# A two-layer graph network on one core: the residual pieces of h, the zero fills, the first search step and the tile words

## The chip, the cores and the metric

The program runs on one core of a Trainium2 chip. The time is the device time of one execution in microseconds (us); the runs before gave 5438.78 us as the median of three (5437.1 to 5440.79).

## The reference

`x` is a table of 12500 nodes by 64 values, `src` and `dst` are 412500 edges, sorted by `dst`. LN is a layer norm without weights (eps 1e-5).

```
h    = relu(LN(x))
x1   = x + relu(h @ W_self + mean over the edges into a node of h[src] @ W_neigh + b)
h    = relu(LN(x1))
e    = sigmoid(relu([h[src], h[dst]] @ We1 + be1) @ We2 + be2)      # one gate per edge
m    = e * h[src]
msgs = [segment_max(m, dst), segment_sum(m, dst)]
out  = x1 + relu([msgs, h] @ Wn1 + bn1) @ Wn2 + bn2 + h
```

`h + ...` in the last line is the residual inside the second network, and `x1 + ...` the outer one.

## The kernel before, in words

The nodes lie in T = 98 tiles of P = 128. Each engine has a program of its own, and the order of the work is written out by hand with semaphores; nothing is planned by a scheduler. A loop made by `in_one_block` is a loop on one engine. The stages in order of time:

- **Search (0 to 180 us).** For each node the place of its first edge in `dst` is sought. ScalarE (L1577, loop of SITER = 10 steps of PASS = 10 columns, entered after `act.wait_ge(s_q, 2)`) counts with Sign activations in which row of 625 entries the place lies. VectorE turns the counts into row numbers (`rows_of`, L954 and L955; `stage_rows`, L958), GpSimd gathers these rows (L580), and VectorE counts inside them (`count`, L964). `search_step(it)` first takes all ten columns of step it + 1 with one `rows_of`, then counts step it, two columns at a time, and stages the rows of the next. It is called for step 0, in a loop with the moments of x (L981), and once behind it. Before and beside it the SP queue brings x (L742, L743) and copies `src` (L746 to L749).
- **Sort (180 to 380 us).** GpSimd gathers each node's list of sources (L580, `runs`), 14 halves of 7 tiles; VectorE masks each half (L1042, L1045, L1047), sorts the first 32 entries (L1055, L1059) and writes it (L1064, L1065). SP stores each half to `sorted_rows` (L761). Two halves stand ahead of a loop and two behind it. At the start SP waits for `s_start` and fills `extra_rows` (L751) and `ranked_rows` (L753) with zeros from SBUF.
- **h and its pieces.** ScalarE makes h of layer 0 in 14 groups (L1606), rounds each to bf16 as the first piece (L1611) and stores h (L1612). The second piece is the rounded rest, the third the rounded rest of the rest: GpSimd subtracts (L602), ScalarE rounds (L1616), GpSimd subtracts again (L607), each for two halves of 49 tiles. In GpSimd's program they stand behind all gathers of the sort. Only the sums of layer 0 (L1867) use the pieces.
- **Ranking (380 to 440 us).** VectorE counts how many sources of each node lie in early tiles (L1094, L1095), bins the nodes by how many are left, and ranks them by a one-hot matrix of 64 bins by 98 tiles (L1111), a scan (L1113), and its product with the offsets (L1128, L1130) summed over the bins (L1131). `row_at` (L1141) lets GpSimd scatter the rows by rank (L613, 98 scatters).
- **Tile words (440 to 455 us).** On one partition VectorE works out per tile how many slots and blocks it has and where they begin (`word_sums`, `rounded_up`, L1149 to L1195), into `ctl`. Then it raises `s_ctl`, for which SP (ahead of the first edge load of layer 0), GpSimd and TensorE wait.
- **Layer 0 (455 to about 2170 us).** 49 steps q of two phases. VectorE builds one-hot matrices of source ids (L1286), TensorE makes counts of them (L1859), ScalarE evicts these (L1627), TensorE multiplies them with the pieces of h (L1867), and the node part follows (`mean_of` L1292 to L1299, `new_x` L1305, `new_h`). The one-hot matrices of a phase begin only when TensorE has transposed the next ids (L1849), which in turn waits until the phase before has been built. VectorE's steps 0 to 4 are written out, the rest are loops. From step 5 on the words of the tiles serve to pack the late rows (`take_late`, L1253). SP loads the late rows and the ids of the early ones (`load_late`, L829) between `next_tiles(4)` and `next_tiles(5)`.
- **Behind it** GpSimd gathers the rest of the early rows (to 2430 us), then layer 1 runs tile by tile to the end.

## Time and profile before

| | |
|---|---|
| median of 3 runs | 5438.78 us |
| the profiled execution | 5435.6 us |
| its span | 5433.9 us |
| VectorE busy | 4035.2 us (74%) |
| GpSimd busy | 3687.3 us (68%) |
| ScalarE busy | 2774.4 us (51%) |
| TensorE busy, matmuls | 2013.7 us (37%) |
| mean granted TensorE clock | 0.697 |

A share is an average over stages that have different limits; what an edit is worth is read from its own stage. In a row of the timeline the first number is the start, the second the duration, then engine (PE TensorE, DVE VectorE, ACT ScalarE, POOL GpSimd, SPq the queue of SP) and line, and in brackets the time for which the engine was idle just before and what ended it; "issue" is a wait for nothing that the profile shows. The granted clock of 1.00 is 2.4 GHz and 0.50 is 1.2 GHz; between them it is a mean of stretches at the two.

### The profile page before, as it was taken

The numbers are of one execution on the slowest core, as the hardware profiler recorded it, in microseconds if no ns is written. First come the engines' busy times: TensorE is split into PE (matmuls) and PEld (weight loads), VectorE is DVE, ScalarE is ACT, GpSimd is POOL, SyncE is SP. The second block draws the span as 40 slices with busy tenths as digits, with TensorE's granted clock in tenths as the row PEclk, the third lists the DMA queues.
The fourth block names the chain that finished last, engine by engine and source line by source line (L and its number), as shares of the span: only waits on it lengthen the run. The fifth ranks groups of instructions, "written<-read, shape, count | busy, mean of one in ns | idle before, by whom it ended". The sixth has DMA issues, their size and how long they took to land.

```text
span 5433.9 us, 105141 instructions
## 1 busy us (share of the span) xinstructions
PE 2013.7 (37%) x18241; PEld 1777.4 (33%) x18241; DVE 4035.2 (74%) x8508; ACT 2774.4 (51%) x7285; POOL 3687.3 (68%) x3830
## 2 busy tenths in 40 slices
PE   0005899999999998000111111111111111111110
PEld 0004888888888888000000000101011111111110
DVE  6788788888888886006777778878888888887770
ACT  7304777887888886003444444444445444544440
POOL 5545216777777777767777777777777777766547
PEclk9999999999999999555555555555555555555555
DMA  7610315555555555554434444444444444443440
GB/s 212 166 24 27 41 52 173 160 160 158 163 160 160 158 163 167 158 156 101 124 113 124 124 122 125 124 133 126 132 133 135 133 142 136 142 134 118 123 98 24
DMA packets 491280, 696.11 MB, mean 128 GB/s; under 512 B 249885, under 2 KB 339843, under 8 KB 491163
## 3 DMA queue, kind: packets, MB, share of 16 engines
q0 software_dynamic: 181472, 381.28, 26.1%
q1 hardware_dynamic: 228085, 172.05, 10.3%
q10 hardware_dynamic: 81638, 141.95, 7.8%
q14 instruction: 69, 0.57, 0.0%
q8 instruction: 16, 0.26, 0.0%
HBM read 513.68 MB, written 163.18 MB: 125 GB/s over the span
## 4 chain that ended last, share of the span: by engine, by line
PE 22%; issue 20%; POOL 19%; DVE 17%; DMA 8%; ACT 7%; ACTq 4%; DVEq 3%; POOLq 0%; SPq 0%
POOL counts_f L580 13%; PE ps_acc L1867 10%; PE ps L1859 9%; DMA counts_f<-early_rows 5%; POOL extra_f L580 4%; DVE act_w L1450 4%; ACT counts_f L1627 3%; DMA counts_f<-hA_table,stage 2%; DVE pre L1444 2%; DVE run_max L1467 2%; ACT msg L1726 1%; DVE z L1456 1%; POOL out_dram L727 1%; ACTq L1726 1%; DVE pre L1059 1%
## 5 line engine op out<-in xcount | busy, mean ns | idle before, releaser
L580 POOL DMA_INDIRECT counts_f<-hA_table,stage x2144 | 2070.9, 966 | 794.3 <-issue 632.1
L1627 ACT ACTIVATE counts_f<-ps 128x784 bf16<-128x784 f32 x1568 | 1269.3, 823 | 468.6 <-PE ps L1859 385.7
L1444 DVE TENSOR_TENSOR pre<-counts_f,ps 128x512 f32 (+1 forms) x862 | 588.6, 683 | 825.2 <-SPq L897 316.9
L580 POOL DMA_INDIRECT extra_f<-hA_table,estage x984 | 932.1, 947 | 314.4 <-issue 290.4
L1726 ACT ACTIVATE msg<-counts_f,gate (+1 forms) x3448 | 921.5, 337 | 315.9 <-ACT gate L1721 293.8
L1867 PE MATMUL ps_acc<-pieces_f,counts_f 128*128 128x192 bf16 x9604 | 1021.3, 247 | 2.4 <-issue 2.4
L1867 PEld LDWEIGHTS ps_acc<-pieces_f,counts_f 128*128 128x128 bf16 x9604 | 885.7, 138 | 3.3 <-issue 2.8
L1859 PE MATMUL ps<-hot 128*128 128x196 bf16 x6272 | 820.6, 253 | 127.0 <-ACT counts_f L1627 106.5
L1938 PE MATMUL ps_acc<-ident,h_tile 128*64 128x128 f32 x98 | 38.6, 394 | 2210.3 <-DVE cat L1503 2210.3
L1721 ACT ACTIVATE gate<-z,be_col (+1 forms) x862 | 256.2, 297 | 1165.1 <-DVE z L1456 820.5
L1938 PEld LDWEIGHTS ps_acc<-ident,h_tile 128*64 128x64 f32 x98 | 12.6, 129 | 2226.4 <-issue 2226.4
L1286 DVE TENSOR_TENSOR hot<-ps_t,iota_hi 128x3136 bf16<-128x3136 bf16 x392 | 698.1, 1781 | 0.0
L1859 PEld LDWEIGHTS ps<-hot 128*128 128x128 bf16 x6272 | 534.2, 98 | 217.9 <-issue 190.6
L1450 DVE SCALAR_TENSOR_TENSOR act_w<-pre,ps 128x512 f32<-128x512 f32 x862 | 586.1, 680 | 0.1
L1456 DVE TENSOR_REDUCE z<-act_w 128x512 f32 x862 | 585.2, 679 | 0.5 <-DVE act_w L1450 0.5
L1286 DVE TENSOR_TENSOR hot<-ps_t,iota_lo 128x2048 bf16<-128x2048 bf16 x392 | 479.2, 1222 | 105.4 <-PE ps_t L1849 70.5
L1467 DVE TENSOR_TENSOR run_max<-run_max,msg 128x256 f32<-128x256 f32 x764 | 322.8, 423 | 6.7 <-ACT msg L1726 6.7
L638 POOL DMA_INDIRECT own_rows<-node x98 | 97.3, 993 | 281.5 <-ACT node L1638 238.1
L1476 DVE TENSOR_TENSOR run_sum<-run_sum,msg 128x256 f32<-128x256 f32 x666 | 279.0, 419 | 0.0
L580 POOL DMA_INDIRECT extra_f<-hA_table,pieces_of x192 | 181.5, 945 | 58.5 <-issue 58.5
L1943 PE MATMUL ps<-catT,w_n1a 128*128 128x128 f32 x196 | 75.1, 487 | 384.1 <-ACT hT L1748 355.6
L1943 PEld LDWEIGHTS ps<-catT,w_n1a 128*128 128x128 f32 x196 | 49.1, 312 | 420.5 <-issue 420.5
(231 smaller groups left out, 2853.5 us busy)
## 6 DMA issues: line engine op xcount, KB each, us to landing
early_rows<-extra_f SPq DMA_DIRECT2D x294, 384.0 KB
counts_f<-early_rows ACTq DMA_DIRECT2D x98, 1152.0 KB
counts_f<-hA_table,stage POOLq DMA_INDIRECT x2144
counts_f<-counts_f SPq DMA_DIRECT2D x67, 288.0 KB
extra_f<-hA_table,estage POOLq DMA_INDIRECT x984
own<-own_rows ACTq DMA_DIRECT2D x98, 130.0 KB
hA_table<-node ACTq DMA_DIRECT2D x98, 96.0 KB
ranked_rows<-zeros SPq DMA_DIRECT2D x1, 3724.0 KB, 50.4
```

What stands on the lines that cost most here:

```text
L580: return pool.indirect_dma_start(to, None, table, bass.IndirectOffsetOnAxis(ap=idx, axis=axis))
L1286: v.tensor_tensor(hot[:, s & 1, :, :, :], ids.unsqueeze(2).to_broadcast(shape), iota.unsqueeze(1).to_broadcast(shape), ALU.is_equal).then_ ...
L1444: v.tensor_tensor(pre[:, :, :], rows[:, :, D:WROW], ps_b[:, bass.ds(i & 1, 1), :].to_broadcast([P, SLOTS, H]), ALU.add).then_inc(s_pre, 1)
L1450: v.scalar_tensor_tensor(out=act_w[:, :, :], in0=pre[:, :, :], scalar=0.0, in1=bc_mid(ps_we2, SLOTS), op0=ALU.max, op1=ALU.mult).then_inc( ...
L1456: v.tensor_reduce(of_two(z, w).rearrange("p a s -> p (a s)"), act_w[:, :, :], AX.X, ALU.add).then_inc(s_z, 1)
L1467: v.tensor_tensor(run_max[:, :, :], run_max[:, :, :], messages(w), ALU.max).then_inc(s_cmax, 1)
L1476: v.tensor_tensor(run_sum[:, :, :], run_sum[:, :, :], messages(w), ALU.add).then_inc(s_acc, 1)
L1627: act.activation(counts[:, c, nodes, :].rearrange("p (b h) t -> p b (h t)", h=2), ps_pairs[g & 1][:, :].rearrange("p (b w) -> p b w", b=BA ...
L1721: act.activation(gate[:, bass.ds(w & 1, 1), :], z[:, bass.ds(w & 1, 1), :], ACT.Sigmoid, bias=be2_col[:, 0:1]).then_inc(s_gate, 1)
L1726: last = act.activation(msg[:, bass.ds(w & 1, 1), s, :].rearrange("p a d -> p (a d)"), rows[:, s, 0:D], ACT.Copy, scale=gate[:, bass.ds(w ...
L1859: last = pe.matmul(ps_pairs[g & 1][:, i * (BANK // 2):i * (BANK // 2) + 2 * T], hot_lo[:, (g // 4) & 1, at // 2, :, at % 2], hot_hi[:, (g ...
L1867: last = pe.matmul(ps_acc[c][:, 0:PIECES * D], counts[:, c, :, t], pieces[:, t, :], start=t == 0, stop=t == T - 1)
```

## The change

Six edits, all in front of the fifth step of layer 0.

1. ScalarE's wait for `s_q` stands inside its search loop instead of ahead of it.
2. The first search step counts two columns first, then takes the rows of the two columns of the next step, then stages them; the other steps stay as they are.
3. The zero fills stand behind the twelfth of the 14 stores of sorted halves, not ahead of the first; the loop of stores has one turn less, and that turn stands behind the fills.
4. The second and third piece are made by TensorE and ScalarE in 14 groups, right behind h: TensorE adds the identity times h and minus the identity times the pieces in PSUM, ScalarE rounds. GpSimd's four subtractions are gone.
5. The sum over 64 bins is a tree of six additions in place of one reduction.
6. The tile words leave their place. Those of the extra blocks (`ctl` 8 and 9) are made while the first gathers of the sort are under way; the others, `late_words`, between VectorE's phases (3, 1) and (4, 0) of layer 0. A new semaphore `s_places` tells SP (ahead of `load_late`), GpSimd (ahead of its early gathers) and ScalarE (ahead of layer 1).

```diff
+            pool.wait_ge(s_places, 1)                      # GpSimd, ahead of the early gathers
-            pool.wait_ge(s_first, 2 * TITER)
-            for h in range(2):
-                pool.tensor_tensor(x_nodes[half], h_nodes[half], pieces[half, 0:D], ALU.subtract)
-            for h in range(2):
-                pool.wait_ge(s_sec, h + 1)
-                pool.tensor_tensor(pieces[half, 2 * D:3 * D], x_nodes[half], pieces[half, D:2 * D], ALU.subtract)
...
-            sp.wait_ge(s_start, 1)
+            with in_one_block(sp, 0, TITER - 1) as it:
+                store_sorted(it)
             sp.dma_start(extra_rows..., zeros...)
             sp.dma_start(ranked_rows..., zeros...)
-            with in_one_block(sp, 0, TITER) as it:
-                ...
+            store_sorted(TITER - 1)
...
             sp.wait_ge(s_recw, 16 * T)
+            sp.wait_ge(s_places, 1)
             for h in range(2):
                 load_late(0, h)
...
-            search_step(0)
+            for a in range(PARTS):
+                at = slice(PASS + a * PCOLS, PASS + (a + 1) * PCOLS)
+                count(0, a)
+                rows_of(at, PASS + (a + 1) * PCOLS)
+                stage_rows(at, a)
...
+            rounded_up(node_deg[:, :], RUN, crow[:, 2, :], 1)       # behind thr, ahead of the sort
+            st.link(v.tensor_scalar(crow[:, 2, :], crow[:, 2, :], -1.0, 1.0, ALU.add, ALU.max))
+            word_sums(crow[:, 2, :], 8)
...
-            v.wait_ge(s_piece, 2)
+            v.wait_ge(s_piece, 2 * TITER)                           # ahead of the one-hot L1111
...
-            st.link(v.tensor_reduce(cols2[:, :], order.rearrange("p b t -> p t b"), AX.X, ALU.add))
+            half = BINS // 2
+            while half > 1:
+                at = order_flat[:, 0:half * T]
+                st.link(v.tensor_tensor(at, at, order_flat[:, half * T:2 * half * T], ALU.add))
+                half //= 2
+            st.link(v.tensor_tensor(cols2[:, :], order_flat[:, 0:T], order_flat[:, T:2 * T], ALU.add))
...
+            def late_words():
+                ...                                                 # the words 0 to 7, as they were
+                v.memset(crow[:, 3, :], 0.0).then_inc(s_places, 1)
+                v.wait_ge(s_places, 1)
+            phase(3, 0)
+            phase(3, 1)
+            late_words()
+            phase(4, 0)
+            phase(4, 1)
...
-            act.wait_ge(s_q, 2)
             with in_one_block(act, 0, SITER) as it:
+                act.wait_ge(s_q, 2)
...
+            def second(g):
+                act.wait_ge(s_rest, max(1, 2 * g))
+                act.activation(tiles_of(g, 1), rest_in(g), ACT.Copy).then_inc(s_sec, 1)
+            def third(g):
+                act.wait_ge(s_rest, min(2 * g + 3, 4 * TITER))
+                act.activation(tiles_of(g, 2), rest_in(g), ACT.Copy).then_inc(s_piece, 1)
+            second(0)
+            for g in range(1, 2 * TITER):
+                second(g)
+                third(g - 1)
+            third(2 * TITER - 1)
...
+            def rest(g):                                            # TensorE
+                if g >= 2:
+                    pe.wait_ge(s_piece, g - 1)
+                pe.matmul(bank, ident[:, :], h_nodes[:, at, :], start=True, stop=False)
+                pe.matmul(bank, minus_b[:, :], pieces[:, at, 0:D], start=False, stop=True).then_inc(s_rest, 1)
+            def rest_of_rest(g):
+                pe.wait_ge(s_sec, g + 1)
+                ...                                                 # the two of rest(g) again, and
+                pe.matmul(bank, minus_b[:, :], pieces[:, at, D:2 * D], start=False, stop=True).then_inc(s_rest, 1)
+            pe.wait_ge(s_first, 2 * TITER)
+            rest(0)
+            for g in range(1, 2 * TITER):
+                rest(g)
+                rest_of_rest(g - 1)
+            rest_of_rest(2 * TITER - 1)
```

Here `at` are the 7 tiles of group g, `bank` is bank g & 1 of `ps_4`, and `rest_in(g)` the same bank. `minus_b` is a new constant, minus the identity in bf16.

## Rows read from the trace of the kernel before

**Rows 1.** The chain of waits, 0 to 760 us: start, length, what.

```profile
13.89 8.02 issue
...
187.46 5.97 DMA runs<-src_pad,tstage
...
334.81 25.06 DVE valid L1042
...
426.34 11.86 DVE cols L1131
...
628.51 3.18 issue
```

**Rows 2.** The timeline of the search: start, duration, engine, line; idle before and releaser in brackets.

```profile
13.26 0.50 DVE L941 CAST hot<-own 128x660 f32<-128x660 int32 x1 [9.02 <-DMA own<-dst_top]
...
22.02 1.28 ACT L1577 ACT_TABLE_LOAD   x1 [21.88 <-issue]
...
25.63 0.17 DVE L958 CAST sstage<-row 128x2 int32<-128x2 f32 x1
...
26.84 1.17 POOL L580 DMA_INDIRECT extra_f<-in_dst_dram,sstage  x1 [24.00 <-issue]
...
52.37 1.28 ACT L1577 ACT_TABLE_LOAD   x1 [0.43 <-ACT hot L1577]
...
53.09 0.17 DVE L954 TENSOR_SCALAR row<-balance  x1 [0.69 <-issue]
```

**Rows 3.** A stretch of the search: busy time per engine, clock, DMA share, GB/s.

```profile
20.00:25.00 5.00, 0.00 (x0) 0.00 (x0) 0.00 (x0) 2.97 (x6) 0.00 (x0) 1.00 1.12 218
```

**Rows 4.** The timeline where the sort begins.

```profile
179.31 19.13 SPq L753 DMA_DIRECT2D ranked_rows<-zeros  x1
...
193.55 0.39 DVE L1045 SCALAR_TENSOR_TENSOR pre<-valid,runs 128x224 f32<-128x224 f32 x1 [8.94 <-DMA runs<-src_pad,tstage]
...
220.49 0.63 DVE L1042 TENSOR_TENSOR valid<-iota_run,deg 128x448 f32<-128x448 f32 x1 [6.68 <-issue]
```

**Rows 5.** The gathers of L580 from 165 us on: landing times.

```profile
DMA to landing us min/median/max: 2.3/2.5/8.3
```

**Rows 6.** The mask of the sort, L1042, by its line.

```profile
L1042 DVE TENSOR_TENSOR valid<-iota_run,deg x14: 617/626/25046, 184.0 to 369.8; 128x448 f32<-128x448 f32 x14
```

**Rows 7.** The stretch of the long mask; busy times of PE, PEld, DVE, ACT, POOL in turn.

```profile
335.00:360.00 25.00, 0.00 (x0) 0.00 (x0) 24.85 (x1) 5.63 (x2) 24.33 (x5) 1.00 0.05 10
```

**Rows 8.** The timeline of ScalarE at the end of its h loop.

```profile
222.54 0.58 ACT L1611 ACTIVATE pieces_f<-counts_f  x1 [0.21 <-ACT counts_f L1606]
```

**Rows 9.** The timeline of the ranking and the tile words.

```profile
419.62 6.69 DVE L1130 TENSOR_TENSOR counts_f<-counts_f 128x6272 f32<-128x6272 f32 x1
...
441.10 0.20 DVE L1173 TENSOR_SCALAR crow<-crow 1x98 f32<-1x98 f32 x1
...
447.10 0.24 DVE L1165 TENSOR_SCALAR crow<-node_deg 1x98 f32<-1x98 f32 x1
...
450.36 0.24 DVE L1165 TENSOR_SCALAR crow<-crow 1x98 f32<-1x98 f32 x1
...
454.82 0.06 DVE L1195 MEMSET std<- 128x1 f32 x1
```

**Rows 10.** The timeline of VectorE and TensorE in layer 0.

```profile
555.57 0.23 DVE L1305 SCALAR_TENSOR_TENSOR node<-ps_y,xh 128x64 f32<-128x64 f32 x1 [0.19 <-PE ps_y L1889]
...
564.40 1.36 PE L1859 MATMUL ps<-hot 128*128 128x196 bf16 x8 [3.00 <-issue]
...
576.70 0.23 DVE L1305 SCALAR_TENSOR_TENSOR node<-ps_y,xh 128x64 f32<-128x64 f32 x1 [0.88 <-PE ps_y L1889]
...
593.64 0.23 DVE L1305 SCALAR_TENSOR_TENSOR node<-ps_y,xh 128x64 f32<-128x64 f32 x1 [0.57 <-PE ps_y L1889]
...
595.89 1.22 DVE L1286 TENSOR_TENSOR hot<-ps_t,iota_lo 128x2048 bf16<-128x2048 bf16 x1 [1.32 <-PE ps_t L1849]
```

**Rows 11.** A stretch of layer 0 behind a pause of TensorE; columns as in Rows 3.

```profile
565.00:580.00 15.00, 14.06 (x141) 12.96 (x140) 7.96 (x10) 10.98 (x17) 8.70 (x10) 0.90 0.14 43
```

More of the change, by code:

```diff
@@ L182, in gnn_kernel @@
         ident_b = sb("ident_b", [P, P], BF16)
+        minus_b = sb("minus_b", [P, P], BF16)
         upper = sb("upper", [P, P])
@@ L404, in gnn_kernel @@
         s_ctl = sem("s_ctl")
+        s_places = sem("s_places")
         s_tidx = sem("s_tidx")
@@ L749, in _, with store_sorted @@
             sp.dma_start(flat_src[E:E + SRC_PAD].unsqueeze(0), src_tail[0:1, :]).then_inc(s_tab, 16)
-            sp.wait_ge(s_start, 1)
+            sorted_by_tile = sorted_rows.rearrange("(t p) w -> p t w", p=P)
+            def store_sorted(it):
+                for h in range(2):
+                    wait_alone(sp, s_srt, 4 * it + 2 * h + 2)
+                    tiles_at = bass.ds(it * (2 * THALF) + h * THALF, THALF)
+                    sp.dma_start(sorted_by_tile[:, tiles_at, :], rows_sb[:, tiles_at, :]).then_inc(s_srtw[h], 16)
+            with in_one_block(sp, 0, TITER - 1) as it:
+                store_sorted(it)
             sp.dma_start(extra_rows.rearrange("(t p) d -> p t d", p=P),
@@ L943, in _ @@
             st.done(v.tensor_copy(ident_b[:, :], ident[:, :]))
+            st.done(v.tensor_scalar(minus_b[:, :], ident[:, :], -1.0, None, ALU.mult))
             st.done(v.tensor_copy(iota_lo2[:, :, :], bc(iota_p[:, :], 2)))
@@ L1190, in _ @@
-            st.link(v.tensor_scalar(crow[:, 1, :], crow[:, 2, :], float(-SLOTS), float(SLOTS), ALU.mult, ALU.add))
-            st.link(v.tensor_tensor(crow[:, 0, :], crow[:, 0, :], crow[:, 1, :], ALU.add))
-            st.link(v.tensor_copy(ctl[:, :, 7], crow[:, 0, :]))
-            st.link(v.tensor_scalar(crow[:, 2, :], crow[:, 2, :], float(ECHUNKS), None, ALU.add))
-            word_sums(crow[:, 2, :], 5)
             v.memset(std[:, :], 0.0).then_inc(s_ctl, 4)
@@ L1352, in phase @@
                     take_late(late, c, range(4, THALF), places)
+            def late_words():
+                st.link(v.tensor_scalar(crow[:, 1, :], crow[:, 0, :], float(LATE_MIN), None, ALU.max))
+                word_sums(crow[:, 1, :], 0)
+                halves = crow[:, 3, :].rearrange("p (h t) -> p h t", t=THALF)
+                st.link(v.tensor_tensor(crow[:, 2, :].rearrange("p (h t) -> p h t", t=THALF), halves,
+                                        halves[:, :, 0:1].to_broadcast([1, T // THALF, THALF]), ALU.subtract))
+                st.link(v.tensor_tensor(crow[:, 2, :], crow[:, 2, :], merge_max[:, :], ALU.min))
+                st.link(v.tensor_copy(ctl[:, :, 4], crow[:, 2, :]))
+                rounded_up(crow[:, 0, :], RUN, crow[:, 2, :], 1)
+                word_sums(crow[:, 2, :], 2)
+                rounded_up(crow[:, 1, :], SLOTS, crow[:, 2, :], 3)
+                st.link(v.tensor_copy(crow[:, 0, :], ctl[:, :, 1]))
+                st.link(v.tensor_tensor(crow[:, 0, :], crow[:, 0, :], crow[:, 1, :], ALU.add))
+                st.link(v.tensor_scalar(crow[:, 1, :], crow[:, 2, :], float(-SLOTS), float(SLOTS), ALU.mult, ALU.add))
+                st.link(v.tensor_tensor(crow[:, 0, :], crow[:, 0, :], crow[:, 1, :], ALU.add))
+                st.link(v.tensor_copy(ctl[:, :, 7], crow[:, 0, :]))
+                st.link(v.tensor_scalar(crow[:, 2, :], crow[:, 2, :], float(ECHUNKS), None, ALU.add))
+                word_sums(crow[:, 2, :], 5)
+                v.memset(crow[:, 3, :], 0.0).then_inc(s_places, 1)
+                v.wait_ge(s_places, 1)
             PER_Q = 10
@@ L1361, in _ @@
             phase(2, 1)
-            for q in range(3, 5):
-                phase(q, 0)
-                phase(q, 1)
+            phase(3, 0)
[3 more added lines that the diff above has]
+            phase(4, 1)
             first = st.now()
@@ L1612, in _, with rest_in, tiles_of @@
                 act.dma_start(h0_by_tile[:, tiles_at, :], h_nodes[:, tiles_at, :]).then_inc(s_h0w, 16)
-            for h in range(2):
-                half = slice(h * (T // 2), (h + 1) * (T // 2))
-                act.wait_ge(s_rest, h + 1)
-                act.activation(pieces[:, half, D:2 * D], x_nodes[:, half, :], ACT.Copy).then_inc(s_sec, 1)
+            def rest_in(g):
+                return ps_4[:, (g & 1) * BANK:(g & 1) * BANK + THALF * D].rearrange("p (t d) -> p t d", d=D)
+            def tiles_of(g, k):
+                return pieces[:, g * THALF:(g + 1) * THALF, k * D:(k + 1) * D]
+            def second(g):
[9 more added lines that the diff above has]
+            third(2 * TITER - 1)
             act.wait_ge(s_w, W_DMAS)
@@ L1801, in tile @@
                     done(before + n)
+            act.wait_ge(s_places, 1)
             act.activation(ps_we2, we2_rows[:, :], ACT.Copy).then_inc(s_second, 1)
```

70 lines of the change are left out of this document (25 added, 45 removed).

## The prediction

> **What bounds the kernel now.** I read the chain of waits first, cut to the first 760 us, since all six edits end there. The span is 5433.9 us and the profiled execution 5435.6 us. Up to the first load of edges for layer 0 the stages follow one another with one engine at work at a time, nearly always VectorE, so what is taken off the chain there comes off the end. Five links of the chain stand out [rows 1]: 8.02 us of "issue" at 13.89, where no engine works; 5.97 us for a gather to land at 187.46; 25.06 us of one mask on VectorE at 334.81; 11.86 us of a reduction at 426.34; and 3.18 us of "issue" at 628.51, inside layer 0. Then I took the timeline around each link and around each place that the edits move work to. Behind layer 0's fifth step nothing is edited, and its order hangs on semaphores of that step and later ones: GpSimd's early gathers are paced by the one-hot matrices, layer 1 begins behind them. I let the shift at that step pass to the end unchanged.
>
> **Edit 1, ScalarE's wait moved into its loop.** The words of `dst` are ready at 13.26 + 0.50 = 13.76, and ScalarE begins at 22.02 [rows 2]. The 8.02 us between follow the wait, at the point where the loop is entered. GpSimd has its wait inside its loop: its first index is ready at 25.63 + 0.17 = 25.80 and it starts at 26.84, 1.0 us later [rows 2]. In the gap the x load holds the DMA engines full, share 1.12 [rows 3]. I read the gap as code brought in by DMA behind that load, and with the wait inside it is brought in during the first microseconds. ScalarE then starts at about 13.9: gain 8.1. Ends: 0, if the gap belongs to something else; 9.4, if its table load (1.28) goes ahead of the wait too.
>
> The Trainium skill (Runtime: NRT & Kernel Launch, section "Instruction fetch mechanics") says that a taken branch to code outside the small window of fetched pages stops the engine until a DMA has fetched the page. By that rule the gap goes, as I have it; without it, nothing on the rows would name the gap and the sum would be 8.1 smaller. No row here shows the fetch itself.
>
> What collides: the first ten gathers now run beside the x load. They must have landed before VectorE can finish step 0. With DMA at share 1.12 until both are through I expect VectorE done with step 0 at 41 to 44, against the 43.9 at which it is wanted. I take no loss and keep 3 us of it for the range.
>
> **Edit 2, counts first.** VectorE ends step 0 with the cast ahead of 53.09 [rows 2], because it began only when all ten Signs of step 1 were there. With counts first it would end some 6 us sooner, but step 1 is unchanged and needs ten Signs of step 2, which ScalarE ends 0.43 us ahead of 52.37, at 51.94 [rows 2]. So 53.09 becomes 52.1: gain 1.0, not 6. From there on VectorE is the dense one. Ends 0 and 1.0.
>
> **Edit 3, the zero fills.** They are issued at 179.31, and the issue of the larger alone takes 19.1 us [rows 4]. The two have 7.0 MB (98 x 128 rows of 256 and of 304 bytes); with the 3.2 MB of h stored meanwhile, at the 218 GB/s of a full stretch [rows 3], they fill the DMA engines for some 47 us, to about 226. In that time two things on the chain are late. The first gathers are late: VectorE goes on at 193.55 after 8.94 us of waiting [rows 4], the last 5.97 of them for the seventh gather to land [rows 1]; the median gather lands in 2.5 us, the slowest in 8.3 [rows 5]. 6.0 becomes 2.5: gain 3.4 (ends 0 and 3.4). And VectorE enters its sort loop at 220.49 after 6.68 us of "issue" [rows 4]; entering the loop of layer 0, with DMA nearly idle, costs 3.18 [rows 1]. Gain 3.5 (ends 0 and 6.0). The fills then start at about 320 and last 32 us at that rate, at most 40, to 360. What is queued behind them on SP: the last two stores of sorted halves, first needed at the edge load near 398. What runs beside them: the last gathers, issued before; VectorE's last two halves, written out without a loop. In the old place the same load stood over two halves written out as well, from 193.55 on, and the wait came only at 213.81 (220.49 - 6.68), where the loop begins. So I price the new place at 0; its cover is 40 us of ranking.
>
> **Edit 4, the pieces.** The mask L1042 takes 0.63 us in the median of 14 and 25.05 once [rows 6]. The long one lasts from 334.81 to 359.87 [rows 1]; from 335 to 360 GpSimd is busy for 24.33 us [rows 7], which are its four subtractions, placed behind the last gather, and VectorE begins nothing else. It stood while GpSimd worked. Gain 25.05 - 0.62 = 24.4. Ends: 24.4 and 23, since nothing else was waiting. What comes in their place: TensorE starts when the last first piece is there, 222.54 + 0.58 [rows 8], 9 us sooner after edits 1 and 2, so at 214, and ScalarE has nothing else. Per group ScalarE rounds twice, 0.58 each for the same 448 columns [rows 8]; matmuls of this shape aren't in the trace, so I bound a group between 1.2 and 6 us. 14 groups end between 231 and 298; VectorE asks at about 350. Price 0.
>
> **Edit 5, the tree.** An addition of 6272 columns takes 6.69 us [rows 9], the mask's 448 columns 0.617 [rows 6]: 1.043 ns a column and 0.15 fixed. The six additions have 3136 + 1568 + 784 + 392 + 196 + 98 = 6174 columns: 6.44 + 0.90, and 0.2 between them, 7.5 us. The reduction goes, 11.86 [rows 1]: gain 4.3 (ends 3.5 and 4.6).
>
> **Edit 6, the tile words.** From 441.10 to 454.82, 13.7 us, go from the chain [rows 9]. Words 8 and 9, 447.10 to 450.36 = 3.3 us, go into VectorE's 8.94 us of waiting, of which edit 3 leaves 5.5: price 0. The other 10.5 us stand between two phases of layer 0. There VectorE has 1.32 us of waiting for transposed ids [rows 10] and no lead beyond it, because it may not build the next phase early. So 9.2 us are late, and TensorE runs dry. What a pause costs beside itself is seen where TensorE stood for 3.00 us ahead of 564.40: the node step of that phase comes 21.1 us after the one before (576.70 - 555.57), its usual distance being 16.9 (593.64 - 576.70) [rows 10], thus 4.2 for 3; the granted clock is 0.90 over the next 15 us, that is 3 us at the level of 1.2 GHz and 1.5 lost [rows 11]. I take 9.2 + 1.6 = 10.8. Ends: 8, if TensorE's backlog covers more; 14.8, at the ratio of 4.2 to 3. Net gain 13.7 - 10.8 = 2.9 (ends -1.1 and 5.7). SP's wait for `s_places` puts the late loads and the id loads behind them some 9 us later, as late as VectorE itself, so the next x loads keep their distance. GpSimd's scatters start with `row_at` and layer 0 comes 13 us nearer to them, 98 scatters with the own rows of the first tiles between them; I see no row of layer 0 that waits for them and leave this to the range.
>
> The Trainium skill (TensorE: Matmul & The Clock Gate, section "What's actually happening") says that the throttled clock is the default and activity releases it. By that rule a longer pause costs no more clock than a short one once it has fallen, the 1.5 us that the rows give; without it a pause three times as long could cost 4.5, and the sum would be 3 smaller.
>
> **The sum.** 8.1 + 1.0 + 3.4 + 3.5 + 24.4 + 4.3 + 2.9 = 47.6. The profiled execution goes from 5435.6 to 5388.0. It lies 3.2 under the median of the runs shown, so the median goes from 5438.8 to 5391.
>
> **Rivals.**
> - *ScalarE's gap stays* (edit 1 does nothing, edit 2 keeps its 1.0): 5391 + 8.1 = 5399. For it: the profile does not name the gap. Against it: GpSimd's 1.0 us. 0.13.
> - *The fills meet VectorE again.* The load arrives as VectorE leaves the loop at 320; if that costs it what entering did, up to 6.9 us return: 5398. For it: same engine, same load. Against it: the 20 us from 193.55 to 213.81 under the old load, without such a wait. 0.15.
> - *The change does not do what it says with the pieces*: TensorE and ScalarE are not through when VectorE asks. That needs over 9 us a group; at 12 us a group 14 x 12 = 168 us end at 382, some 32 late: 5423. Against it: 0.58 us a rounding. 0.02.
> - *The other side: TensorE does not get its clock back* after the long pause in layer 0. Each microsecond at 1.2 GHz loses half of one. It eats the gain after 95 us and is slower by 0.2% after 117; 200 us give 5391 + 100 = 5491. Against it: full clock again within the stretch of 15 us [rows 11]. For it: the pause is three times as long. 0.03. The Trainium skill (TensorE: Matmul & The Clock Gate, section "Seeing it yourself") tells of a clock stuck at a low level for over 50 us; no run here shows it.
> - The forecast: 0.67.
>
> **Chances and range.** About 0.2% (11 us) is what a measurement of this kernel tells from no change. Faster needs less than 5428: all cases but the last, and some allowance for a wait in layer 0 that I do not see: 0.94 faster, 0.04 within, 0.02 slower. The ends of the terms add to gains of 27 and 54; all of them at one side is unlikely, and the rivals that hold chance reach 5399. Range 5380 to 5404.
>
> **What would show it.** In the trace after: ScalarE's first Sign at about 15 instead of 23; VectorE's second search step at 44; the first sorted half begun near 181; no L1042 over 1 us; the end of the sort near 340; `row_at` near 396; first one-hot matrix near 403 (460 before, so 57 in front of layer 0, 10 of which go back at its fourth step). The forecast is wrong if ScalarE still starts at 22, if idle time over 3 us stands on VectorE between 320 and 400, or if layer 0 from its first one-hot matrix to its end grows by more than 15 us or less than 6.

## The result, and the profile after

The kernel after takes 5380.73 us (median of 4 runs, 5380.55 to 5381.06), the kernel before 5437.94 in the same measurement (4 runs, 5433.44 to 5440.79): ratio 0.9896, 95% interval 0.9878 to 0.9913. It is faster by 1.04%. The forecast was 5391 with a range of 5380 to 5404; the direction holds, and so do all terms in front of layer 0 except those of edits 1 and 2 together. The total lies 0.7 us inside the lower end of the range, because layer 0, which was to give back 10.8 us, gave back nothing, and 2.2 us were lost behind it. The profiled spans are 5433.9 and 5378.9, 55.0 us apart, and this difference is what is taken apart below.

The timeline of the kernel after, in front of layer 0 (start, duration, engine, line; idle before and its releaser in brackets):

```profile
13.83 1.28 ACT L1588 ACT_TABLE_LOAD   x1 [13.69 <-DVE hot L935]
...
28.89 0.87 DVE L959 TENSOR_SCALAR_CACHE_REDUCE hot<-extra_f,q_node 128x625 bf16<-128x625 int32 x1 [4.66 <-DMA extra_f<-in_dst_dram,sstage]
...
35.19 0.87 DVE L959 TENSOR_SCALAR_CACHE_REDUCE hot<-extra_f,q_node 128x625 bf16<-128x625 int32 x1 [3.60 <-DMA extra_f<-in_dst_dram,sstage]
...
46.52 0.48 DVE L976 BATCH_NORM_STATS2 runs<-counts_f  x2 [0.39 <-DVE row L950]
...
182.47 0.41 DVE L1069 SCALAR_TENSOR_TENSOR pre<-valid,runs 128x224 f32<-128x224 f32 x1 [3.10 <-DMA runs<-src_pad,tstage]
...
206.02 0.63 DVE L1066 TENSOR_TENSOR valid<-iota_run,deg 128x448 f32<-128x448 f32 x1 [3.27 <-issue]
...
320.30 0.62 DVE L1066 TENSOR_TENSOR valid<-iota_run,deg 128x448 f32<-128x448 f32 x1 [0.30 <-DVE extra_f L1089]
...
321.31 14.53 SPq L752 DMA_DIRECT2D ranked_rows<-zeros  x1
...
387.41 7.26 DVE L1158 TENSOR_TENSOR counts_f<-counts_f 128x3136 f32<-128x3136 f32 x5
394.70 0.26 DVE L1160 TENSOR_TENSOR cols<-counts_f 128x98 f32<-128x98 f32 x1
...
403.03 1.23 DVE L1271 TENSOR_TENSOR hot<-ps_t,iota_lo 128x2048 bf16<-128x2048 bf16 x1 [0.67 <-PE ps_t L1902]
```

ScalarE starts at 13.83 (22.02 before, [rows 2]); its releaser is now the cast of the words of `dst` and no longer "issue". The first key comes at 182.47 (193.55, [rows 4]), the first mask of the loop at 206.02 (220.49, [rows 4]), and the long mask of [rows 1] takes 0.62 us. All 14 masks are alike:

```profile
L1066 DVE TENSOR_TENSOR valid<-iota_run,deg x14: 624/625/649, 178.7 to 330.8; 128x448 f32<-128x448 f32 x14
```

The same instructions have these starts in both traces. The shift is what the kernel after is ahead at that point, the gain is what the stretch gave:

| point | before | after | shift | gain | predicted |
|---|---|---|---|---|---|
| first step with x (bn_stats) | 54.03 | 46.52 | 7.51 | 7.51 | 9.1 |
| `start` ready | 178.41 | 170.91 | 7.50 | 0 | 0 |
| first key of the sort | 193.55 | 182.47 | 11.08 | 3.58 | 3.4 |
| first mask of the loop | 220.49 | 206.02 | 14.47 | 3.39 | 3.5 |
| first one-hot of the ranking | 389.62 | 350.68 | 38.94 | 24.47 | 24.4 |
| `row_at` | 439.63 | 396.40 | 43.23 | 4.29 | 4.3 |
| first one-hot of layer 0 | 460.19 | 403.03 | 57.16 | 13.93 | 13.7 |
| last node step of layer 0 | 2166.65 | 2109.49 | 57.16 | 0.0 | -10.8 |
| end of the span | 5433.9 | 5378.9 | 55.0 | -2.2 | 0 |

Inside layer 0 the node steps show where the 10.8 did and did not come. A node step is VectorE's instruction `new_x` for one tile; there are 98, one per phase, and from here on "step" with a number is one of these 98 and not one of the 49 steps q. The words stand ahead of the ninth phase and hold up node step 7, since the node part comes two phases late. Rows of the timeline of the kernel after, node steps 4 to 7 (those of [rows 10] are 4 to 6), and TensorE at the pause:

```profile
495.48 0.23 DVE L1290 SCALAR_TENSOR_TENSOR node<-ps_y,xh 128x64 f32<-128x64 f32 x1 [0.34 <-PE ps_y L1942]
...
505.03 0.52 PE L1912 MATMUL ps<-hot 128*128 128x196 bf16 x4 [1.97 <-ACT counts_f L1654]
...
514.62 0.22 DVE L1290 SCALAR_TENSOR_TENSOR node<-ps_y,xh 128x64 f32<-128x64 f32 x1 [0.88 <-PE ps_y L1942]
...
531.57 0.22 DVE L1290 SCALAR_TENSOR_TENSOR node<-ps_y,xh 128x64 f32<-128x64 f32 x1 [0.57 <-PE ps_y L1942]
...
545.59 1.46 PE L1912 MATMUL ps<-hot 128*128 128x196 bf16 x8 [8.19 <-DVE hot L1271]
...
559.06 0.23 DVE L1290 SCALAR_TENSOR_TENSOR node<-ps_y,xh 128x64 f32<-128x64 f32 x1 [0.85 <-PE ps_y L1942]
```

From step 6 to step 7 are 27.5 us; before they were 17.0. This is the pause of the tile words, 10.5 us, as the sum had it. Nearly everything else in layer 0 went the other way: the first step is 2.8 us nearer to the first one-hot than before, the fifth 2.0 nearer to the fourth (19.1 after the fourth, 21.1 before), and between steps 9 and 22 come 3.6 more. The rest drifts by 0.7 to step 96 and 1.6 at the last two steps. Only step 9 gives 0.4 away. So at the last node step the kernel after is as far ahead, 57.16 us, as at the first one-hot: layer 0 takes as long as before, with the words in it. Behind it 2.2 us are lost.

### The profile page after: what moved, and what is told of

Same layout as the page of the kernel before. It is cut to its first block, busy times and chain, and to the rows that moved or that the text cites. A ratio compares the mean times of both kernels' runs of the same rounds, so it can differ in the third digit from the quotient of the medians.

```text
span 5378.9 us, 105382 instructions
## 1 busy us (share of the span) xinstructions
PE 2043.1 (38%) x18339; PEld 1787.8 (33%) x18339; DVE 4007.2 (74%) x8523; ACT 2784.3 (52%) x7311; POOL 3665.1 (68%) x3826
## 3 DMA queue, kind: packets, MB, share of 16 engines
q1 hardware_dynamic: 228085, 172.05, 10.5%
## 4 chain that ended last, share of the span: by engine, by line
PE 22%; POOL 22%; issue 20%; DVE 15%; DMA 9%; ACT 6%; ACTq 3%; DVEq 3%; POOLq 0%; SPq 0%
POOL counts_f L581 16%; PE ps_acc L1920 10%; PE ps L1912 9%; DMA counts_f<-early_rows 5%; POOL extra_f L581 4%; DVE act_w L1461 3%; ACT counts_f L1654 3%; DMA counts_f<-hA_table,stage 2%; DVE pre L1455 2%; DVE run_max L1478 2%; DVE z L1467 1%; ACT msg L1753 1%; POOL out_dram L717 1%; DVE pre L1083 1%; DVE hot L959 1%
```

## The experiments

The twelve runs, in three groups of four, were made on two chips on which this program is 40% slower than in the first measurement: the kernel before takes 7636 and 7756 us (the first and second group, one chip) and 7641 us (the third, another). Two controls of the kernel after stand at ratios of 0.9974 and 0.9947, each known to about 0.16%; that is 25 and 43 us below the kernel before, where the first measurement has 57. Totals tell nothing under 10 us there, so each question is read from its own stage, in most cases from one trace. e3, e5 and e8 have a single execution each (7607.5, 7614.9 and 7610.6 us). The search runs nearly as in the first measurement (from bn_stats to `start` ready 124.4 to 129.0 us, 124.4 there), the ranking and steps 5 to 17 of layer 0 as well; the sort's loop and the rest of layer 0 don't.

### ScalarE's wait, and what the 8 us are (e2, e3)

e2 is the kernel after with edit 1 undone:

```diff
+            act.wait_ge(s_q, 2)
             with in_one_block(act, 0, SITER) as it:
-                act.wait_ge(s_q, 2)
```

> The kernel after, with edit 1 alone undone: ScalarE's wait stands ahead of its loop again. Theory (code is fetched at the loop entry, behind the x load): ScalarE's table load starts at 22.0 again and not at 13.8, VectorE's first step with x data (bn_stats, 46.5 in the kernel after) at 53 to 54, and the time is 5380.7 + 6.5 to 7.5 = 5387 to 5388. Rival (the early start came with another edit, by a shift of the code or by the counts first): table load at about 13.8 to 15, time 5381 to 5382.

e3 adds one line, ahead of the load of x on SP:

```diff
+            sp.wait_ge(s_bal, 1)
             sp.dma_start(x_nodes[:, 0:FULL, :], ...)
```

> The run before this one (wait ahead of ScalarE's loop) with one more edit: SP holds the load of x until ScalarE's first Sign is done, so the DMA engines are nearly idle when ScalarE enters its loop. Theory (the 8 us are a fetch that queues behind the x load): the table load starts 1 to 3.5 us after the words of dst are ready, at 14.8 to 17.3. Rival (the wait ahead of a loop costs ScalarE 8 us whatever the DMA engines do): it starts at 22 as before. In both the time says little, since x itself comes later.

The timeline of e2, then that of e3:

```profile
22.31 1.28 ACT L1588 ACT_TABLE_LOAD   x1 [22.17 <-issue]
...
55.93 0.48 DVE L976 BATCH_NORM_STATS2 runs<-counts_f  x2 [0.39 <-DVE row L950]
```

```profile
16.04 1.28 ACT L1589 ACT_TABLE_LOAD   x1 [15.90 <-issue]
```

With the x load away the gap is 2.65 us (in e3 the words of `dst` are ready at 13.39), with it 8.30 (in e2 they are ready at 14.01). The DMA view names the transfer itself, on a queue called "instruction" (packets, MB, share of the engines). In the kernel before the only packet between 10 and 26 us lies between 18 and 20:

```profile
q1 hardware_dynamic: 422, 0.43, 111.7%
q14 instruction: 1, 0.01, 1.8%
```

In e2 the only one between 10 and 26 lies between 20 and 26, in e3 the first between 14.3 and 15.0:

```profile
q14 instruction: 1, 0.01, 3.6%
```

In the kernel after none lies between 10 and 26, and two between 3 and 6. So the gap is code fetched behind the x load, as forecast: without the load it shrinks by 5.7 us, and a packet of code lies in it each time. The time of e2, 7618 (ratio 0.9976, 0.9963 to 0.9988), is too close to the controls to price the 8 us; the search does: `start` is ready at 180.35, against 171.2 to 174.3 in the runs with ScalarE early and the load of src in its place.

### Counts first (e8)

The kernel after with edit 2 undone:

```diff
-            for a in range(PARTS):
-                at = slice(PASS + a * PCOLS, PASS + (a + 1) * PCOLS)
-                count(0, a)
-                rows_of(at, PASS + (a + 1) * PCOLS)
-                stage_rows(at, a)
+            search_step(0)
```

> The kernel after, with edit 2 alone undone: VectorE waits for all ten Signs of step 1 before it counts anything of step 0. Theory as predicted (counts first is worth 1 us, because step 1 still needs ten Signs of step 2): the first step with x data (bn_stats) at 47.5 to 48 and not 46.5 to 47.0. Rival (with ScalarE early, ScalarE's Signs no longer bound step 0 but VectorE's counts and the gathers do, so counts first is worth the counting it moves forward): bn_stats at 50 or later.

At bn_stats neither. The step comes sooner without the edit:

```profile
33.77 0.17 DVE L949 TENSOR_SCALAR row<-balance 128x10 f32<-128x10 f32 x1 [9.49 <-ACT hot L1584]
...
45.34 0.48 DVE L976 BATCH_NORM_STATS2 runs<-counts_f  x2 [0.39 <-DVE row L950]
...
54.19 0.17 DVE L953 CAST sstage<-row 128x2 int32 x1 [1.92 <-issue]
...
63.10 0.17 DVE L949 TENSOR_SCALAR row<-balance  x1
```

From ScalarE's table load to bn_stats are 31.46 us here (45.34 - 13.88). In the seven runs with counts first and ScalarE early they are 32.14 to 32.72 (e10, below, has less for another reason), and 32.69 in the kernel after of the first measurement. With ScalarE late it is the same: 33.62 in e2, with counts first, 32.01 in the kernel before, without. Up to bn_stats edit 2 costs 0.7 to 1.6 us. The rows show why: with rows first one pair of instructions makes the ten rows, and by the time it is done the ten gathers have all landed; with counts first each of five parts has its own pair (2.40 us a part in place of 1.87), and the first two wait 4.66 and 3.60 us for gathers.

But e8 does not keep this. Its next search step takes 18.5 us (44.57 to 63.10), and in all runs with counts first 14.8 to 15.8. VectorE's idle times there, 0.88, 1.15 and 1.92, all go by "issue". The control of the same group, c2, begins the step behind it at

```profile
61.47 0.17 DVE L949 TENSOR_SCALAR row<-balance  x1
```

and e5 at 60.94, so e8 is 1.6 and 2.2 us behind them by then, and its `start` is ready at 174.31, against 171.96 and 171.27. On this chip counts first is therefore worth 2.4 and 3.0 us at the end of the search, one trace against two. e4, the kernel before on the other slow chip, has the long step as well (18.2 us). On the chip of the first measurement it is not there: 14.96 us in the kernel before, 14.78 in the kernel after. GpSimd begins the gathers for that step at 37.13 in e8 and at 33.13 in c2; whether the long step comes from that was not tested, and what edit 2 gave on the first chip stays open.

### The zero fills (e5)

The kernel after, the two fills put back behind `start` and ahead of SP's loop (the wait `sp.wait_ge(s_start, 1)` and the two dma_start of `zeros`, as the diff of edit 3 shows them removed).

> The kernel after, with edit 3 alone undone: the two zero fills are issued behind `start` again, ahead of SP's loop. Theory (the fills hold the DMA engines while VectorE wants the first gathers and the code of its sort loop): VectorE waits about 9 us less the 3.3 that words 8 and 9 now fill, thus 5.5 to 6 and not 3.1, for the first gathers, and the loop's first mask comes some 3 us later still than that. From the end of the search (`start` ready) to that mask: 35 us in the kernel after on the first chip (206.0 - 170.9), 37.0 in c1 on the other; by the theory 7 us more. Rival (the gain between those two points came from edit 4 or 6, not from the fills): no more than in the kernel after.

```profile
172.16 18.34 SPq L743 DMA_DIRECT2D ranked_rows<-zeros  x1
...
186.43 0.39 DVE L1070 SCALAR_TENSOR_TENSOR pre<-valid,runs 128x224 f32<-128x224 f32 x1 [6.70 <-DMA runs<-src_pad,tstage]
```

The wait for the first gathers is 6.70 in place of 3.02 (c2), 3.74 (c1) and 3.10 (the kernel after), and from `start` ready to the first key are 15.16 us, against 11.5 to 12.2 in the two controls, 11.56 in the kernel after and 15.14 in the kernel before in the first measurement. So the half of edit 3 at the first gathers is shown, 3.0 to 3.7 us.

The half at the loop entry is not. The expectation compares two different masks: 206.02 in the kernel after is the third, the first one in the loop; the 37.0 us of c1 end at the second, ahead of the loop. Up to the second mask e5 has 36.8 us and its control c2 36.0. The third stands here:

```profile
225.86 0.63 DVE L1067 TENSOR_TENSOR valid<-iota_run,deg 128x448 f32<-128x448 f32 x1 [3.12 <-issue]
```

Its 3.12 us are the same in c2. But the two halves ahead of the loop take longer on these chips, and the fills are through by then (76 GB/s from 221 to 228 us, 244 from 214 to 221 in the kernel before), so e5 does not put the load on the loop entry. The 3.39 us rest on the two traces of the first measurement (6.68 and 3.27 of "issue"); in both, and in e5, one packet of the queue "instruction" lies inside that wait.

### The pieces (e1)

The kernel after with GpSimd's four subtractions back behind the last gather, ScalarE rounding two halves, and TensorE's fourteen groups gone:

```diff
+            pool.wait_ge(s_first, 2 * TITER)
+            for h in range(2):
+                pool.tensor_tensor(x_nodes[:, half, :], h_nodes[:, half, :], pieces[:, half, 0:D], ALU.subtract)
...
-            rest(0)
-            for g in range(1, 2 * TITER):
-                rest(g)
-                rest_of_rest(g - 1)
-            rest_of_rest(2 * TITER - 1)
```

> The kernel after, with edit 4 alone undone: GpSimd makes the pieces of h again with its four subtractions, behind the last gather. Theory (VectorE's mask stands as long as GpSimd works on the same core): the mask at about 320 takes 25 us and the time is 5380.7 + 24.4 = 5405. Rival (the other edits moved GpSimd's gathers so that its subtractions fall elsewhere, or VectorE slows down but doesn't stand): mask under 10 us and the time under 5393.

```profile
346.30 24.86 DVE L1077 TENSOR_TENSOR valid<-iota_run,deg 128x448 f32<-128x448 f32 x1 [0.30 <-DVE extra_f L1100]
```

GpSimd's subtractions on the same trace:

```profile
346.34 12.19 POOL L603 TENSOR_TENSOR counts_f<-counts_f,pieces_f 128x3136 f32<-128x3136 f32 x2
358.49 12.18 POOL L608 TENSOR_TENSOR pieces_f<-counts_f,pieces_f 128x3136 bf16<-128x3136 f32 x2
```

The mask begins with GpSimd's first subtraction and ends 0.5 us behind its last: 24.86 us, where the median of the 14 masks is 0.63. The time, 7631, has a ratio of 0.9993 (0.9984 to 1.0003), above both controls, as it should be, without being a measure of 24 us.

### The tile words in layer 0 (c1, c2, e6, e7)

c1 and c2 are the kernel after itself, as the level on this chip.

> The kernel after as it is, because the chip of the first four runs took 7636 us for the kernel before and not 5438: loops of TensorE, ScalarE and VectorE stand 6 to 9 us per pass there in layer 0 and in the sort. If this call's chip is like the first measurement, 5381 (ratio 0.9896); if it is like the second, this gives the level that the runs e1, e2 and e7 are to be read against: by theory (each takes back what its edit gave) 7636 less about 45 = 7590, thus e2 above it by 9, e1 by 25 or more.

> The kernel after as it is, for the level of this call (the kernel before took 7636 in the first call and 7756 in the second, on the same chip). By the first measurement it is 57 us below before on a chip of the first kind; on the other it was 25 below, with intervals of 0.15%. Theory: 25 to 57 below before.

e6 puts the late words ahead of layer 0 again:

```diff
+            late_words()
             v.memset(std[:, :], 0.0).then_inc(s_ctl, 4)
...
-            late_words()
             phase(4, 0)
```

> The kernel after, with the late tile words ahead of layer 0 again (10.5 us and the release of s_ctl behind them); words 8 and 9 stay in the wait for the first gathers. Theory (moving them inside was worth nothing, since they cost there what they cost here): first one-hot matrix 10.5 us later at 413.5, no 10.5 us hole in the node steps at the seventh, and the time 5380 to 5382 (the same as after within 1). Rival, as predicted (a pause inside costs more than its length, by TensorE's clock): the time is lower than after's by 0.3 to 4. Other rival (TensorE's backlog covers part of the pause inside): the time is higher by 1 to 3.

e7 keeps them in layer 0, but in pieces:

```diff
+            some_words()
             phase(0, 1, mean=False, last=False)
+            some_words()
             phase(1, 0, last=False)
...
             phase(3, 1)
-            late_words()
+            words_done()
             phase(4, 0)
```

Here `some_words()` issues the next five instructions of the list.

> The kernel after, but the late tile words (38 instructions, 10.5 us in one piece behind the seventh phase's last step) in pieces of five instructions of about 1.2 us, one ahead of each phase from the second on, where VectorE waits 0.7 to 1.6 us for transposed ids; the rest and the release of s_places stand where they stood. Theory (the words cost 10.5 us there because they are one piece, and TensorE's backlog or VectorE's waits cover small ones): the seventh node step stays at the shift of the sixth (62 and not 51.6 against the kernel before), and 2 to 9 us stay to the end: 5372 to 5379, likeliest 5375. Rival (VectorE has no slack in a phase, its waits follow its own lateness): each piece is late by its own length and the shift falls by about 1.2 a phase to the same 51.6, time 5380 to 5382.

> The same kernel as e7_words_spread. On a chip where the kernel before takes 5438: theory 5372 to 5379 and the seventh node step at a shift of about 62 against the kernel before; rival (no slack in a phase) 5380 to 5382 and the shift falling to 51.6 by then. On a chip where it takes 7636, by the theory 2 to 9 us below the kernel after of this call, by the rival the same.

Steps 5 to 8 are a stretch without the stops of the slow chips. Steps 6 and 7 of c1:

```profile
689.10 0.22 DVE L1290 SCALAR_TENSOR_TENSOR node<-ps_y,xh 128x64 f32<-128x64 f32 x1 [0.57 <-PE ps_y L1942]
...
716.74 0.22 DVE L1290 SCALAR_TENSOR_TENSOR node<-ps_y,xh 128x64 f32<-128x64 f32 x1 [0.86 <-PE ps_y L1942]
```

and of the second run of e7:

```profile
693.48 0.23 DVE L1295 SCALAR_TENSOR_TENSOR node<-ps_y,xh 128x64 f32<-128x64 f32 x1 [0.46 <-PE ps_y L1963]
...
710.50 0.22 DVE L1295 SCALAR_TENSOR_TENSOR node<-ps_y,xh 128x64 f32<-128x64 f32 x1 [0.86 <-PE ps_y L1963]
```

The distance from step 6 to step 7 is 27.6 in c1, 27.0 in c2, 17.0 in e6 and in both runs of e7. The pause costs its own 10.0 to 10.6 us and nothing behind it: step 7 to 8 is 17.0 in all of them. Whether the small pieces cost anything is seen from the first one-hot matrix to step 8: 274.5, 275.5 and 276.5 us in the three runs with words spread (e7 twice, e10), 282.9 to 285.5 with the words in one piece (c1, c2, e2, e3, e5, e8; e1 has 290.6). Spread, they take 6 to 11 us less of this stretch. That says little for the first chip: six of the seven small pieces lie ahead of step 5, where TensorE stops on these chips (from step 2 to 5 a step takes 32 to 36 us in place of 17), so that VectorE has time in plenty. Only two steps are undisturbed. Step 5 to 6 has one piece of five instructions in it and takes 17.13 us, against 16.94 to 16.96 without; step 6 to 7 has the last three and takes 17.02, as in e6 without any. So where a phase runs at full pace VectorE did have slack for 1.2 us, and my rival fell there; that ten microseconds of words fit in this way was not measured on an undisturbed chip. In e6 the stretch takes 267.4, and with the 10.8 us ahead of it 278.2; that is less than c1, but its first phases lie among the stops of the slow chip, which shift against them, so I don't take the 7 us for a gain. The totals don't decide it: in the second group 7719.9 for e7 (0.9961, 0.9945 to 0.9977) and 7721.3 for e6 (0.9955, 0.9942 to 0.9969) against 7730.6 for c1 (0.9974, 0.9958 to 0.9989); the intervals overlap. The first run of e7, 7595.5 (0.9943, 0.9929 to 0.9957), has no control in its group.

### Where TensorE's code lies (e4)

The kernel before with idle instructions at the start of TensorE's program:

```diff
+            for _ in range(100):
+                pe.sem_inc(s_passed, 1)
             pe.wait_ge(s_const, 9)
```

> The kernel before, with 100 idle instructions (semaphore increments that nobody waits for) ahead of TensorE's first wait. They end long before TensorE is asked for anything, so by themselves they cost nothing. Theory (TensorE's stops of 1.8 us at 491 and of 3.0 at 564, and their smaller successors in the kernel after, depend on where TensorE's code lies): one or both stops change by 1 us or more, and the node steps of layer 0 shift by as much against the kernel before, to either side by up to 3 us: 5435 to 5441. Rival (they belong to the work, not to the place of the code): both stops stand as they were, 5438.

TensorE stops in straight-line code, waiting for nothing. The kernel before, in the first measurement:

```profile
491.00 0.45 PE L1859 MATMUL ps<-hot 128*128 128x196 bf16 x3 [1.80 <-issue]
...
502.56 0.43 PE L1859 MATMUL ps<-hot 128*128 128x196 bf16 x3 [0.26 <-issue]
```

and e4:

```profile
583.42 0.52 PE L1861 MATMUL ps<-hot 128*128 128x196 bf16 x4 [1.80 <-issue]
...
595.00 0.34 PE L1861 MATMUL ps<-hot 128*128 128x196 bf16 x2 [0.87 <-issue]
```

Counted from layer 0's first transpose, the stops of the kernel before stand behind 189 and 308 matmuls, those of e4 behind 262 and 381, in both 119 apart. A matmul is two instructions with its weight load, so 100 more instructions ahead pull a boundary forward by 50: 308 becomes 258, and 262 is where it stands; 381 is the next. The places of the stops moved with the code, by about the amount of the code. Their lengths did not go with them: the boundary that cost 0.26 us in the kernel before costs 1.80 in e4. The DMA view has packets of the instruction queue beside them:

```profile
q8 instruction: 1, 0.02, 2.6%
```

is the one between 580 and 583 us of e4, just ahead of its stop. The Trainium skill (Runtime: NRT & Kernel Launch, section "Instruction fetch mechanics") says that code comes in blocks of 256 instructions and that the crossing of a block is mostly hidden. The distance of 119 pairs, with the semaphore instructions between them, agrees with it. Mostly hidden it is here too: of the crossings between 488 and 550 us in the kernel before one cost 1.80 us, one 0.26, and no other stop over 0.2 is seen. In the kernel after, whose TensorE program is longer by the piece matmuls, no such stop stands in the first 600 us of layer 0. The 3.00 us at 564 stand at a loop's entry, and this run does not decide them. The time of e4 is 7753 (ratio 1.0002, 0.9988 to 1.0017), no difference that this chip can tell.

### One more load out of the way (e10)

e7, and SP's load of src held back:

```diff
+            sp.wait_ge(s_bal, 3 * PASS)
             flat_src = src_pad.rearrange("a b -> (a b)")
```

> The words spread as in e7, and one thing more: SP issues the load of src (1.6 MB), which nobody reads before the end of the search, after 30 Signs and not right behind x. In the kernel after VectorE waited 4.66 and 3.60 us for gathers of step 0 that share the DMA engines with both loads. Theory: the gathers of step 0 land sooner, bn_stats moves from 46.5 to about 45.2 (it can't be sooner than 30 Signs from 13.8 on, 44.3), and nothing is lost behind it, since the DMA engines have 28% left during the search; with the words spread the whole is 8 to 12 us below c2 in this call (on a chip as in the first measurement 5370). Rival (the load meets the dense part of the search and slows its gathers): bn_stats sooner but `start` ready no sooner, and 7 to 10 us below c2, from the words alone. Other rival, for the words: no gain in the end, within 3 us of c2.

```profile
44.01 0.17 DVE L950 TENSOR_SCALAR row<-balance  x1 [2.67 <-ACT hot L1610]
...
44.97 0.48 DVE L977 BATCH_NORM_STATS2 runs<-counts_f  x2 [0.39 <-issue]
```

bn_stats comes at 44.97, 1.3 to 2.2 us sooner than in the other runs with counts first, and now ScalarE's Signs end the wait and not the DMA. `start` is ready at 169.78, the earliest of all runs (171.2 to 174.3 in the others with ScalarE early on these chips), so nothing was lost behind it. The time is 7591.7 (0.9944, 0.9930 to 0.9957) against 7597.6 for c2 (0.9947, 0.9930 to 0.9965). By its stages it should beat both kernels by some 10 us; that it does is not shown.

## Why the prediction was right or wrong

- **Edit 1, right.** 8.19 us at ScalarE's start, forecast 8.1, by the cause named; e2 brings the gap back, e3 shrinks it by taking away the x load, and the packet is seen.
- **Edits 1 and 2 together, 7.5 us in place of 9.1.** The step that was wrong stands under "What collides": "I expect VectorE done with step 0 at 41 to 44", "I take no loss". VectorE's last instruction of step 0 ends at 44.97, behind waits of 4.66 and 3.60 us for gathers and with parts of 2.40 us in place of 1.87. The forecast looked at what releases VectorE, the last Sign, and not at the work that a step gains when it is cut into five. Whether edit 2 by itself gained or lost is open. At bn_stats e8 is about 1 us better off without it (31.46 us from ScalarE's start, c2 32.58, e5 32.42), at `start` 2.4 to 3.0 us worse off, and the second figure comes from a long step that the first chip doesn't show. With a part of the collision with the loads taken away, e10 is 1.3 us sooner at least.
- **Edit 3, right in both sizes** (3.58 and 3.39 for 3.4 and 3.5). The first is shown by e5; the second is read from two traces of the first measurement, and that the fills were its cause is not shown. The rival of the fills meeting VectorE again fell: they were issued at 321.31, and the longest idle time of VectorE before the ranking's masks is 0.22 us.
- **Edit 4, right** (24.47 for 24.4), with e1 as the other half. A group of pieces takes 2.97 us at either end of my 1.2 to 6, and the last of 14 was ready at 258.8, 92 us before VectorE asks.
- **Edit 5, right** (4.29 for 4.3): 7.26 + 0.26 for the tree, forecast 7.5.
- **Edit 6, the part outside right** (13.93 for 13.7), **the pause right in sum** (10.5 for 10.8), **the net of layer 0 wrong.** The pause has other parts than forecast. The first one-hot matrix behind the words comes at 542.22, 10.65 us after node step 6, before it was 2.25 [rows 10]: 8.4 us late, forecast 9.2. The other 2.1 were forecast at 1.6, on the view that a longer pause costs no more clock than a short one. It cost more: behind the pause of 3.00 us TensorE worked for 3 us at 1.2 GHz [rows 11], behind this one of 8.19 us for some 6 us (545.6 to about 551.5; columns as in [rows 3]):

```profile
541.00:551.60 10.60, 5.62 (x33) 4.98 (x34) 9.06 (x17) 3.34 (x5) 0.00 (x0) 0.52 1.26 62
```

  The step that failed is the rule under "What bounds the kernel now", "I let the shift at that step pass to the end unchanged", and within the first steps the assumption that the pause is the only thing that changes. The forecast said it is wrong if layer 0 grows by less than 6 us to its end; it grew by 6.0 to step 12 (57.16 - 51.18), and to its end by 0.0. By its own sign the forecast's account of layer 0 is wrong, though the total is in the range. What came in the place of the 10.8, in the traces of the first measurement:
  - 2.8 us in front of step 1. 2.0 of them come where the stop of 1.80 us was; that such stops move with the position of TensorE's code is shown by e4, that this one went for that reason is the reading. The other 0.8, in two parts ahead of the stop and behind it, are open.
  - 2.0 us at the loop entry of step 5. Its 3.00 us [rows 10] became 1.97. On both traces instruction packets lie in front of it. Not tested: on the slow chips this stretch is disturbed.
  - 3.2 us at three of the steps 13 to 21. They are TensorE's clock. In the kernel before all three have a granted clock of 0.91 (two of them shown; busy times as in [rows 7]),

```profile
703.30:722.20 18.90, 16.24 (x158) 15.04 (x157) 14.92 (x26) 12.84 (x20) 0.96 (x1) 0.91 0.25 66
...
740.60:759.50 18.90, 16.18 (x157) 14.79 (x156) 14.91 (x26) 12.68 (x20) 0.96 (x1) 0.91 0.25 67
```

  and the same steps of the kernel after at 1.00:

```profile
652.10:670.00 17.90, 15.10 (x164) 13.99 (x163) 15.04 (x27) 12.76 (x20) 0.97 (x1) 1.00 0.26 70
...
688.20:706.10 17.90, 15.06 (x164) 13.95 (x162) 15.02 (x27) 12.76 (x21) 0.97 (x1) 1.00 0.26 71
```

  This is not a property of the change: c1 and c2 are one and the same kernel, and step 12 to 13 takes 17.9 in the one and 18.9 in the other. A single trace of each kernel can't decide it; it also fits that the runs of the kernel before spread by 7 us.
  - the drift of 0.7 and the 1.6 of the last two steps, the 0.4 given away at step 9, and the 2.2 lost behind layer 0: open.

Sum of the errors: the forecast of the gain was 1.6 too high for the search, 0.4 too low in the rest ahead of layer 0, 8.6 too low from there on (10.8 for layer 0, less the 2.2 lost behind it): 55.0 in place of 47.6. Of the 8.6, 3.2 are a difference of the clock of the kind that c1 and c2, one kernel, show between them. That the errors add up to a median just inside the range, by 0.7 us, is luck.

Two sums of the forecast are off. Its terms in front of layer 0 add up to 58.4 and not to the "57 in front of layer 0" under "What would show it"; that 57.16 was measured is no hit of the sum. And the lower ends of its terms add up to 25.4, not 27. Neither changes the median forecast.

## What to carry to other kernels

Look in the DMA view for packets of the instruction queues beside every gap that is called "issue": a loop entry whose code was fetched while a large load held the DMA engines cost 8 us here, a block of straight-line code once 1.8 us, and a wait put inside the loop hid the first. When a step is cut so that its parts can start sooner, price the instructions that the cut adds on the dense engine, not only the wait that it shortens, and read its worth at the end of the stage: at the first step behind the cut e8 was about 1 us ahead, at the end of the search 2.4 to 3.0 behind. Check that a point compared in two traces is the same instruction by its count in the row, not by its clock time: the same line stood at 206 us in one trace and, one turn earlier, at 208 in another. A serial bookkeeping job put into a pipelined loop in one piece cost its full 10.5 us; a piece of 1.2 us in an undisturbed step cost 0.2. Splitting it is worth a try, but the total of that version was not told apart.

## What was not expected of the hardware

The same programs take 1.4 times as long on two other chips, and not evenly. A stretch of 97 us at the start of layer 0, in the kernel after of the first measurement, then two stretches of c1 (busy us and instructions of TensorE, its weight loads, VectorE, ScalarE, GpSimd; clock; DMA share; GB/s):

```profile
403.00:500.00 97.00, 85.77 (x902) 77.28 (x903) 80.36 (x98) 77.92 (x112) 73.83 (x77) 0.96 0.14 40
```

```profile
451.00:548.00 97.00, 34.29 (x299) 27.37 (x300) 30.43 (x28) 31.41 (x39) 47.91 (x50) 0.60 0.06 18
...
734.00:900.00 166.00, 147.60 (x1562) 137.58 (x1560) 136.92 (x241) 122.40 (x189) 9.72 (x10) 0.98 0.15 42
```

In the first stretch c1 does a third of the matmuls, with stops of 3 to 10 us that the trace puts to "issue" or to an unknown releaser; in the last, where GpSimd issues 10 indirect DMAs and not 50, it runs at full pace. The sort and the early gathers, with GpSimd's indirect DMAs one behind the other, are slow as well. But the search has them too (GpSimd busy for 95 of 159 us) and loses at most 5 us of 124, so they alone don't make it. What does was not tried.
